# First layer of a two-layer block: attention moved by four query tiles against the feed-forward net, and its pieces put between that net's products

## The reference

```
xn = layernorm(x)
q, k, v = xn @ Wq, xn @ Wk, xn @ Wv          # 32 heads of 16, 8 key/value heads, each for 4 query heads
s = softmax(q k^T / 4) v, then @ Wo           # full attention over 512 positions
u = fwht(xn * SU_ug) / 64
h = silu(u @ W_gate.T * c_gate) * (u @ W_up.T * c_up)      # 2048 wide
f = (fwht(h * SU_dp) / 64) @ W_down.T * c_down
x1 = x + s * silu(f)
```

## Time and profile before

| | |
|---|---|
| three runs, median (lowest to highest) | 1391.0 us (1390.41 to 1392.87) |
| profiled execution, own time | 1391.33 us |
| its span | 1389.4 us |
| mean granted clock of TensorE | 0.982 of full speed |
| layer 1's first instruction | at 759.86 us of the span |
| TensorE, VectorE, ScalarE, GpSimd busy | 91%, 76%, 56%, 38% |

### The profile page before, as it was taken

One profiled execution on the slowest core, in us unless ns is written; L12 is line 12 of the kernel. 1 busy time (PEld: TensorE's weight loads), 2 busy tenths in 40 slices (PEclk: granted clock), 3 DMA queues, 4 the chain that ended last, 5 costly groups with the idle time before them and its releaser, 6 DMA issues. The chain is left out here.

```text
span 1389.4 us, 23478 instructions
## 1 busy us (share of the span) xinstructions
PE 1263.2 (91%) x8738; PEld 637.2 (46%) x8738; DVE 1055.3 (76%) x1823; ACT 783.0 (56%) x1308; POOL 524.6 (38%) x434
## 2 busy tenths in 40 slices
PE   4667788888998999998898999999999999999998
PEld 2222233333333333333343555855477555855475
DVE  7765886778887888778863976968956976968946
ACT  5665666666776677667726752355433652355431
POOL 3369865211220132013201663328431573328431
PEclk9898999999999999999999999999999999999999
DMA  6864563577777876877675024001131024001121
GB/s 233 204 143 96 96 107 73 96 145 152 121 117 144 164 122 113 149 160 115 119 260 212 1 59 92 17 31 37 44 72 39 8 59 92 17 31 37 43 43 46
DMA packets 346561, 135.59 MB, mean 98 GB/s; under 512 B 312176, under 2 KB 333392, under 8 KB 343888
## 3 DMA queue, kind: packets, MB, share of 16 engines
q1 hardware_dynamic: 334032, 132.52, 44.1%
q10 hardware_dynamic: 12416, 1.57, 1.0%
HBM read 44.87 MB, written 17.87 MB: 45 GB/s over the span
## 5 line engine op out<-in xcount | busy, mean ns | idle before, releaser
L1157 PE MATMUL bank<-rows,both 128*128 128x512 f16 x1024 | 245.9, 383 | 28.6 <-DVE tg L644 19.8
L638 DVE TENSOR_REDUCE top_n<-vpair 128x1 f32<-128x512 f32 x256 | 164.8, 686 | 102.0 <-PE bank L1126 101.8
L940 ACT ACTIVATE probs<-vpair,top_n 128x512 f16<-128x512 f32 x256 | 164.4, 687 | 109.1 <-DVE top_n L638 109.0
L1171 PE MATMUL bank<-dn,h 128*128 128x512 f16 x768 | 179.8, 383 | 4.3 <-DVE fd L711 2.5
L1157 PEld LDWEIGHTS bank<-rows,both 128*128 128x128 f16 x1024 | 91.3, 98 | 164.8 <-DVE tg L644 43.4
L638 DVE TENSOR_REDUCE top_n<-bank 128x1 f32<-128x512 f32 x256 | 163.7, 682 | 0.0
L940 ACT ACTIVATE probs<-bank,top_n 128x512 f16<-128x512 f32 x256 | 162.9, 690 | 0.0
L454 POOL TENSOR_TENSOR h<-th,h 128x512 f16<-128x512 f32 x61 | 70.5, 1155 | 192.5 <-ACT h L909 192.5
L2239 PE MATMUL bank<-rows,both 128*128 128x512 f16 x512 | 118.5, 382 | 0.0
L1171 PEld LDWEIGHTS bank<-dn,h 128*128 128x128 f16 x768 | 71.5, 99 | 98.3 <-issue 15.9
L2255 PE MATMUL bank<-both,hid 128*128 128x512 f16 x512 | 111.2, 379 | 0.0
(11 more groups left out here) (358 smaller groups left out, 2559.3 us busy)
## 6 DMA issues: line engine op xcount, KB each, us to landing
h<-in_ug SPq DMA_DIRECT2D x8, 1024.0 KB, 6.3
lt_scratch<-big SPq DMA_DIRECT2D x16, 384.0 KB, 2.7
dn<-in_down SPq DMA_DIRECT2D x2, 2048.0 KB, 11.0
x_scratch<-th SPq DMA_DIRECT2D x16, 256.0 KB, 2.7
res<-x_scratch SPq DMA_DIRECT2D x16, 256.0 KB, 4.3
out_x<-res SPq DMA_DIRECT2D x16, 256.0 KB, 2.0
both<-in_w SPq DMA_DIRECT2D x2, 1548.0 KB, 11.8
t_scratch<-tok SPq DMA_DIRECT2D x16, 192.0 KB, 2.1
```

Source lines behind the costliest of these rows:

```text
L638: v.tensor_reduce(top_n[:, i:i + 1], SC_[n % G][:, :], AX.X, ALU.max, negate=True).then_inc(S["max_done"], 1)
L940: a.activation(probs[:, k % TAKEN, j * T:(j + 1) * T], SC_[j][:, :], ACT.Exp, bias=top_n[:, i:i + 1]).then_inc(S["p_ready"], 1)
L1157: mm = pe.matmul(GB[n % 2][:, :], w[:, kt, col:col + P], xnb(b, kt), start=r == 0, stop=r == 2 * KT - 1)
L1171: mm = pe.matmul(bk, h16(ft, r // 2)[:, rows], dn16(ft, r % 2), start=j == 0 and r == 0, stop=j == FT - 1 and r == 2)
```

## The change

- All of attention is issued 8 steps later (`ATT` = 8, `ta = t - ATT`), and in odd instead of even steps: tile n at t = 2n + 9. Transposing DMAs, loads of keys and queries, tokens, division and turning back follow. All four maxima and all four exponentials of a tile now stand in the odd step (before, two exponentials in each).
- TensorE: in an odd step scores (and every second time the weighing) stand ahead of the up product, of which at most one matmul goes first; Hadamard products come after them.
- VectorE: first maximum, gate product, three maxima, up product of the same block. The first three row differences stand between.
- ScalarE: hyperbolic tangent, first exponential, row copy, three exponentials, copy of the turned input, high half. In the preparation the high half thus comes last.
- GpSimd: row differences in odd steps, division with attention.
- Output projections at steps 20, 22, 28, 35 instead of 17, 19 (21 for the last batch), 28, 35; keys at 57 instead of 49; evictions of projections always one step after.
- TEND stays 295: the last tile's scores come at step 263 instead of 254.

```diff
--- before.py
+++ after.py
@@ -32,17 +32,16 @@
 BSTEPS = NKV * STEPS
 SLOTS = 4
 TAKEN = 3
-TOKEN_STEP, DIVIDE_STEP, TURN_BACK = 4, 6, 2
-GATE_AHEAD, DOWN_AHEAD = (4, 3), (1, 0)
-LATE_EVICT = 70
+ATT = 8
+TOKEN_STEP, DIVIDE_STEP, TURN_BACK = 6, 0, 2
 OT = KT + 1
 FFN_STEP = 32
 DOWN_END = (8, 16, 24, 32)
-OUT_STEP = (17, 19, 28, 35)
-OUT_LAST = (17, 21, 28, 35)
+OUT_STEP = (20, 22, 28, 35)
+OUT_LAST = (20, 22, 28, 35)
 NEXT_STEP, EVICT_STEP = 19, 20
 XRES_STEP = (17, 19, 24, 25)
-Q_STEP, V_STEP, K_STEP = 5, 43, 49
+Q_STEP, V_STEP, K_STEP = 5, 43, 57
 TEND = B * BSTEPS + OUT_STEP[-1] + 4
 CHUNKS = (0, 4, 1, 5, 2, 6, 3, 7)
 PREP = -2
@@ -358,8 +357,9 @@
             sp.dma_start(wsd[:, :], d["wscale_dp"].partition_broadcast(P)).then_inc(S["wo_in"], 16)
             for t in range(TEND):
                 b, m = t // BSTEPS - 1, t % BSTEPS
-                if t % 2 == 0 and 0 <= t // 2 - 1 < NU * TT:
-                    turn_probs(t // 2 - 1)
+                ta = t - ATT
+                if ta % 2 == 0 and 0 <= ta // 2 - 1 < NU * TT:
+                    turn_probs(ta // 2 - 1)
                 if t in (1, 5):
                     ft = 8 * (t == 5)
                     sp.dma_start(dn[:, ft:ft + 8, :], d["down"][:, ft:ft + 8, :]).then_inc(S[f"dn_in{ft // 8}"], 16)
@@ -371,10 +371,10 @@
                     sp.dma_start(wo[:, :, :], d["wo"]).then_inc(S["wo_in"], 16)
                 if (t - PREP - 2) % 4 == 0 and 2 <= (t - PREP - 2) // 4 + 2 < NCH:
                     load_chunk((t - PREP - 2) // 4 + 2)
-                if t % STEPS == 6 and t // STEPS + 2 < NU:
-                    load_k(t // STEPS + 2)
-                if t % STEPS == 2 and 1 < t // STEPS + 1 < NU:
-                    load_q(t // STEPS + 1)
+                if ta % STEPS == 6 and 1 < ta // STEPS + 2 < NU:
+                    load_k(ta // STEPS + 2)
+                if ta % STEPS == 2 and 1 < ta // STEPS + 1 < NU:
+                    load_q(ta // STEPS + 1)
                 if b >= 0 and m in XRES_STEP:
                     tt = XRES_STEP.index(m)
                     n = b * TT + tt
@@ -501,10 +501,10 @@
                     pool.wait_ge(S["t_dcol"], 1)
                     pool.tensor_tensor(W["dsc"], W["dsc"], W["ipw"][:, 1:2].to_broadcast([P, D]), ALU.mult).then_inc(S["t_dcol"], 1)
                 fb, fm = (t - 2) // BSTEPS, (t - 2) % BSTEPS
-                if fb < B and fm >= FFN_STEP and t % 2 == 0 and (fb or (fm - FFN_STEP) // 2 >= LOW_FIRST):
+                if fb < B and fm >= FFN_STEP and t % 2 and (fb or (fm - FFN_STEP) // 2 >= LOW_FIRST):
                     low_rows(fb, (fm - FFN_STEP) // 2)
-                if t % STEPS == DIVIDE_STEP and t // STEPS - 1 in POOL_UNITS:
-                    divide(t // STEPS - 1)
+                if (t - ATT) % STEPS == DIVIDE_STEP and (t - ATT) // STEPS - 2 in POOL_UNITS:
+                    divide((t - ATT) // STEPS - 2)
                 if b and m - 2 in out_step(b):
                     residual((b - 1) * TT + out_step(b).index(m - 2))
 
@@ -798,11 +798,19 @@
                     chunk_scales(p)
                 if 0 <= t - PREP - 3 < NCH * KT:
                     low_half(t - PREP - 3)
-                if t > FFN_STEP + 1 and (t - 2) // BSTEPS < B and (t - 2) % BSTEPS >= FFN_STEP and t % 2 == 0:
-                    up_mul((t - 2) // BSTEPS, ((t - 2) % BSTEPS - FFN_STEP) // 2)
-                if t < NU * STEPS and t % 2 == 0:
-                    for j in range(G):
-                        row_max(2 * t + j)
+                ta = t - ATT
+                paired = ta % 2 and 0 <= ta // 2 < NU * TT
+                if paired:
+                    row_max(G * (ta // 2))
+                if b < B and m > FFN_STEP and m % 2:
+                    gate_mul(b, (m - FFN_STEP) // 2)
+                if paired:
+                    for j in range(1, G):
+                        row_max(G * (ta // 2) + j)
+                if t % 2 and 0 <= (t - 3 - FFN_STEP) // 2 < LOW_FIRST:
+                    low_rows((t - 3 - FFN_STEP) // 2)
+                if b < B and m > FFN_STEP and m % 2:
+                    up_mul(b, (m - FFN_STEP) // 2)
                 if t == 1:
                     statistics(3)
                 if t == 2:
@@ -815,16 +823,12 @@
                     half_scale()
                 if t == 30:
                     bound_scales()
-                if b < B and m > FFN_STEP and m % 2:
-                    gate_mul(b, (m - FFN_STEP) // 2)
-                if t % 2 and 0 <= (t - 3 - FFN_STEP) // 2 < LOW_FIRST:
-                    low_rows((t - 3 - FFN_STEP) // 2)
-                if t % STEPS == TOKEN_STEP and 0 <= t // STEPS - 1 < NU:
-                    to_tokens(t // STEPS - 1)
-                if t % STEPS == DIVIDE_STEP and 0 <= t // STEPS - 1 < NU:
-                    divide(t // STEPS - 1)
-                if t % STEPS == TURN_BACK and 0 <= t // STEPS - 2 < NU and t // STEPS % 2:
-                    to_features(t // STEPS - 2)
+                if ta % STEPS == TOKEN_STEP and 0 <= ta // STEPS - 1 < NU:
+                    to_tokens(ta // STEPS - 1)
+                if ta % STEPS == DIVIDE_STEP and 0 <= ta // STEPS - 2 < NU:
+                    divide(ta // STEPS - 2)
+                if ta % STEPS == TURN_BACK and 0 <= ta // STEPS - 2 < NU and ta // STEPS % 2:
+                    to_features(ta // STEPS - 2)
                 if b == B and m == 3:
                     next_stats()
                     weight_max(0)
@@ -991,29 +995,33 @@
                     deviations(3)
                 if t == 3:
                     normalise(3)
-                if t > FFN_STEP + 1 and (t - 2) // BSTEPS < B and (t - 2) % BSTEPS >= FFN_STEP and t % 2 == 0:
-                    high_rows((t - 2) // BSTEPS, ((t - 2) % BSTEPS - FFN_STEP) // 2)
+                ta = t - ATT
+                paired = ta % 2 and 0 <= ta // 2 < NU * TT
+                fb, fm = (t - 2) // BSTEPS, (t - 2) % BSTEPS
                 if b < B and m > FFN_STEP and m % 2:
                     tanh_gate(b, (m - FFN_STEP) // 2)
+                if paired:
+                    exps(G * (ta // 2))
+                if 0 <= fb < B and fm > FFN_STEP and t % 2:
+                    high_rows(fb, (fm - FFN_STEP) // 2)
+                if paired:
+                    for j in range(1, G):
+                        exps(G * (ta // 2) + j)
+                if t in TURN_STEP:
+                    evict_x(KT + TURN_STEP.index(t))
                 if 0 <= t - PREP - 2 < NCH * KT:
                     high_half(t - PREP - 2)
-                if t < NU * STEPS:
-                    exps(2 * t)
-                    exps(2 * t + 1)
-                if t in TURN_STEP:
-                    evict_x(KT + TURN_STEP.index(t))
                 for ft in range(FT):
                     if ABS_AT[ft] == t:
                         magnitudes(ft)
+                if t % 16 == Q_STEP + 1 and t // 16 + 1 < NU // 2:
+                    evict_q(t // 16 + 1)
+                if m == V_STEP + 1 and b + 1 < B:
+                    evict_v(b + 1)
+                if m == K_STEP + 1 and b + 1 < B:
+                    evict_k(b + 1)
                 if t in DN_AT:
                     high_down(DN_AT.index(t))
-                late = 1 if t < LATE_EVICT else 2
-                if t % 16 == Q_STEP + late and t // 16 + 1 < NU // 2:
-                    evict_q(t // 16 + 1)
-                if m == V_STEP + late and b + 1 < B:
-                    evict_v(b + 1)
-                if m == K_STEP + late and b + 1 < B:
-                    evict_k(b + 1)
                 if b and m - 1 in DOWN_END:
                     tanh_down((b - 1) * TT + DOWN_END.index(m - 1))
                 if b == B and m == 9:
@@ -1216,18 +1224,17 @@
             sum_maxima(0)
             for t in range(TEND):
                 b, m = t // BSTEPS, t % BSTEPS
+                ta = t - ATT
+                ahead = 1 if ta % 4 == 1 else 0
                 if t in TURN_STEP:
                     turn_x(KT + TURN_STEP.index(t))
+                ffn(t, 0, ahead)
+                if ta % 2 and 0 <= ta // 2 < NU * TT:
+                    scores(ta // 2)
+                if ta % 4 == 1 and 0 <= ta // 4 - 2 < 2 * NU:
+                    weigh(ta // 4 - 2)
                 if 0 <= t - PREP - 2 < NCH * KT:
                     transform_ug(t - PREP - 2)
-                ahead = 0
-                if t % 2 == 0:
-                    ahead = (DOWN_AHEAD if m < FFN_STEP else GATE_AHEAD)[t // 2 % 2]
-                ffn(t, 0, ahead)
-                if t < NU * STEPS and t % 2 == 0:
-                    scores(t // 2)
-                if t % 4 == 0 and 0 <= t // 4 - 2 < 2 * NU:
-                    weigh(t // 4 - 2)
                 ffn(t, ahead, 2 * KT)
                 if t > 0 and t % 4 == (PREP + 1) % 4 and (t - PREP) // 4 < NCH:
                     sum_maxima((t - PREP) // 4)
```

## The result

The changed kernel takes 1400.19 us (median of five runs, 1398.12 to 1402.42) against 1391.0 for the one before (five runs, 1389.33 to 1393.13): a ratio of 1.0063, 95% interval 1.0045 to 1.0082. It is slower, where 1370 was forecast. The profiled execution has a span of 1399.8 us.

A forecast was written before the change was run, and what follows sets the result against it. TensorE, busy 91% of the span, was taken as the bound, with chains between engines in the preparation and loops in the stages. Terms -10 - 12 - 10 + 0 + 11 = -21 gave 1370 us; 8 in 10 range 1355 to 1396.

The forecast's parts named there:

- term 4: Down stages, moved projections and K: no change, between -1 and +1.5 us a stage.
- term 3: Gate and up tiles: 4.75 us against 4.86, plus a shorter stage entry; 2.5 us gained a stage, 10 in all.
- its sign of being wrong: Gate and up tiles taking over 4.9 us; named as one of the readings that would refute the prediction.
- Terms 1 and 2: Preparation: steps 0 to 7 without attention gain 10 us, steps 8 to 31 with reordered work gain 12.
- term 1: Steps 0 to 7: four tiles and two table loads go, gaining 10 us, least 2.6, most 16.
- Term 5: Tail: TensorE idles 13 us behind VectorE's layer 1 block; net cost 11 us, between 7 and 20.
- Rival A: Trapped tail wins: tail costs 18 us, front and stages give back 8.6, so 1400 us; chance 0.20.
- B: It cancels: the front gives 10 us, stages and turning nothing, the tail costs 11, so 1391 us; chance 0.08.
- C: The front opens up: steps 8 to 31 gain 24 us, gate and up stages 16, so 1352 us; chance 0.20.

The follow-up runs named there:

- k59: The changed kernel with the key projection at step 59 instead of 57, its eviction at 60: 1386.73 us.
- store26: k59 with the third output projection at step 26 instead of 28, so the third token tile's store comes two steps earlier: 1377.5 us.
- att0: The changed kernel without the delay of attention (ATT 0 instead of 8) and with the key projection at step 51 instead of 57: 1384.19 us.
- tail9: The changed kernel with VectorE's block for layer 1 at step 9 of the tail instead of step 3: 1397.99 us.
- g4: As g8, but attention delayed by four steps (ATT 4 instead of 8): 1364.12 us.
- g8: store26 (ATT 8), also with no up matmul ahead of the scores in layer 0's gate and up stages: 1368.32 us.
- g0: As g8, but attention not delayed (ATT 0 instead of 8) and keys moved to match: 1366.54 us.

## Why the prediction was wrong

Steps 33 to 257 were forecast at -10 us (terms 3 and 4) and came at +26 in the profiles. **Two steps failed: term 4, which took the moved evictions at nothing, and term 3, which applied the steady tile to whole stages.** In sum: -10 as forecast, +13.5 for the keys, +9 for the stages' entries, +12 for steps 51 to 69 make about +25. The prices of keys and entries come from experiments, that of steps 51 to 69 from the start times alone.

**Term 4**, "moved projections and K", was costed at 0 between -1 and +1.5 a stage. It looked at which bank a projection needs and at what SyncE issues, and not at what the eviction of a projection waits for. Both ends of that wait were moved, the query load by 8 steps with attention and the key eviction by 7 in batches 1 and 2, and the one step between them was lost. Its measured price is 13.5 us (after against k59). The row that could have warned is `ACT kst <- DMA qk<-qst`, 3.6 us in three waits before: a wait already there. The lost step is not all of it. In batch 0 both stood at step 50 before too, and the wait was 1.3 us; after, both stand at step 58, and it is 5.6. There the new order has all exponentials in odd steps, so nothing stands ahead of the eviction on ScalarE.

**Term 3** (-10) had the steady tile right, 4.76 against 4.75, and left out what a stage has beside it. It was mis-sized at the entry, where 0.7 us a stage was to be gained. The changed order asks for the first up product a step earlier, and the store of x1 is then late; store26 puts that at 9.2 us over three stages. The last gate and up stage, which has no key eviction, shows the term alone: steps 225 to 257 took 79.0 us after (617.3 to 696.3) and about 78.1 before, +0.9 in place of -2.5; in store26 they took 75.6, which is the -2.5. And the first stage was counted like the others, although the down weights are transformed in it: steps 51 to 69 cost 12.5 us more, the third place above. Taken over a whole stage, tiles are far over the 4.9 that the prediction named as its sign of being wrong: (397.87 - 310.53)/16 = 5.46 from step 97 to 129, key wait and entry included (4.97 before). The tile with an up matmul ahead of the scores is 5.0 and not 4.7 (337.89 to 342.88), the one with the weighing 4.28 and not 4.4; the errors cancel in the mean.

**Terms 1 and 2** (-22) were 4 us too small, all of it in term 1: step 9 came 14 us earlier for 10, and steps 9 to 33 gave 12 for 12. Tile 0 came at 47.8 (near 50 expected), tile 12 at 135.5 (139). One table load is left of three. The Trainium skill ("ScalarE: Activation LUTs", What ACT_TABLE_LOAD costs), by which term 1 would have been 12.7, adds a drain; in the timeline of after the load begins 0.02 us behind an activation that ends at 48.46, and shows none:

```profile
47.77 0.69 ACT L894 ACTIVATE both<-bank,suc 128x512 f16<-128x512 f32 x1 [1.01 <-PE bank L1076]
48.48 1.28 ACT L944 ACT_TABLE_LOAD   x1
49.88 0.69 ACT L944 ACTIVATE probs<-vpair,top_n 128x512 f16<-128x512 f32 x1
```

But the reason that term 1 gives, the four absent tiles, is less than half of the start. att0, without any delay, is 7.2 us earlier than before at step 9 and 16.6 at step 33, and the delay adds 9.3. The order within the step was worth more than the four absent tiles.

**Term 5** (+11) came as worked out in its rows: an idle time of 13.20 us ended by an exponential (13 forecast), and from step 257 to layer 1 9 us more than before. That the idle time is what costs the 9 us is not shown: tail9 has none of it and takes 70.4 us from step 257 to layer 1, against 72.6 after and 70.6 in k59, which has it. The block ahead of the last maxima, after:

```profile
704.68 2.47 DVE L766 BATCH_NORM_STATS2 both<-rows 128x6 f32<-128x512 f32 x4 [1.38 <-DMA rows<-x_scratch]
...
717.45 1.27 DVE L638 TENSOR_REDUCE top_n<-vpair 128x1 f32<-128x512 f32 x2
...
718.17 1.28 ACT L944 ACTIVATE probs<-vpair,top_n 128x512 f16<-128x512 f32 x2 [14.14 <-DVE top_n L638]
```

**Rival A** gave 1400, the time measured, by luck: it had the front give 8.6 us, which gave 26, and the tail cost 18, which cost 9; the 26 us lost between are not in it. B needed a front of 10; C's was 34.

**Open.** The 12 us of steps 51 to 69 are in every kernel with the new order, g4 with them (71.4 us). The waits for the shared bank are longer there (13.3 us against 7.7) and the granted clock is lower; which of the moved pieces does it was not tested. They also eat a part of the delay's lead: g8's lead over g0 of 9.9 us at step 33 is 3.9 at step 65.

## What to carry to other kernels

When a group of operations is moved by n steps, list each buffer that it shares with work that moves by another amount, writer and reader, and count the steps between them before and after; a staging buffer that is loaded out in one step and overwritten in the same one puts a DMA's issue and landing on the engine that overwrites it. Price a stage by its whole, with the entry and whatever else runs in it, and not by its steady tile alone. Before moving an idle time away in a tail, ask for the next resource in the same queue: here the vector block, the three buffers and the transposes stood one behind the other. A wait of a few us in the profile before is not a constant: it says which two things are already close, and may be worth removing by itself (3.7 us for one step number here).

## What the runs showed of the hardware

A transposing DMA of one tile's exponentials holds SyncE's queue for 1.7 to 3.6 us in the kernel after (98 of them from 205 to 690 us), and 1.8 to 4.1 in its tail. One issued directly behind two loads of 1.5 MB held it for 11.8 us and landed 14.6 us after its issue, and the three behind it took 2.0 to 2.9 (the kernel with the later block and constants). The four small loads of a unit's queries (16 KB each) take 2.4 to 3.0 us of the queue around the steps shown; each lands 1.8 us after its issue (median). Both stand in one queue, so a copy asked for in a step came too late for an engine that wanted its buffer in the same step: 5.6 to 7.5 us of waiting after.
